# Reordering the start-up of a one-core feature-attention and ternary feed-forward kernel on Trainium2

## The reference

```
def _rfs(xw, ab, AB, gs):
    dot_products = jnp.einsum('...d,rd->...r', xw, ab[:, None] * gs)
    correction = (0.5 * jnp.sum(xw * xw, axis=-1))[..., None] * (ab * ab)
    return 1.0 / math.sqrt(NUM_RFS) * AB * jnp.exp(dot_products - correction)
...
weights = _rfs(input_weights, ab, AB, proj_matrix)
feats = _rfs(x, ab, AB, proj_matrix)
return jnp.einsum('bsr,or->bso', feats, weights)
...
h = jax.nn.silu(_tlin(x, w1_w, w1_s)) * _tlin(x, w2_w, w2_s)
h = jax.nn.gelu(_tlin(h, h1_w, h1_s), approximate=False)
h = jax.nn.gelu(_tlin(h, h2_w, h2_s), approximate=False)
return _tlin(h, w3_w, w3_s)
```

## Time and profile before

| | |
|---|---|
| median of 3 runs | 1315.86 us |
| lowest, highest | 1315.18, 1316.37 us |
| profiled execution | 1315.81 us |
| its span | 1314.0 us |
| TensorE busy with products | 1290.7 us (98%) |
| VectorE, ScalarE, GpSimd busy | 947.4, 750.7, 742.1 us |
| granted TensorE clock, mean | 0.998 |

### The profile page before, as it was taken

How to read it: one execution, slowest core, us unless ns; L and a number is a source line. 1 busy time by engine, 2 the same in 40 slices (tenths; PEclk the granted TensorE clock), 3 DMA queues, 4 the chain that set the end, 5 groups by cost and what they waited for, 6 DMA issues and landing times. The chain is left out here.

```text
span 1314.0 us, 16120 instructions
## 1 busy us (share of the span) xinstructions
PE 1290.7 (98%) x6068; PEld 1067.9 (81%) x6068; DVE 947.4 (72%) x1195; ACT 750.7 (57%) x1004; POOL 742.1 (56%) x705
## 2 busy tenths in 40 slices
PE   6999999999999999999999999999999999999997
PEld 5788888888888888888878888788897888878887
DVE  7887759677587875877758786687857777466575
ACT  3556644666456664566644656456554575555664
POOL 7952014789558994589935998369982791020000
PEclk9999999999999999999999999999999999999999
DMA  9787734654255452555416544274542754313441
GB/s 338 268 314 230 267 97 117 196 175 152 102 133 196 152 180 77 147 169 177 161 69 168 179 148 163 80 185 150 174 133 81 188 177 131 110 64 128 136 166 38
DMA packets 96836, 207.50 MB, mean 158 GB/s; under 512 B 13936, under 2 KB 16240, under 8 KB 95728
## 3 DMA queue, kind: packets, MB, share of 16 engines
q1 hardware_dynamic: 80032, 157.11, 35.9%
q0 software_dynamic: 16720, 49.30, 13.7%
HBM read 174.87 MB, written 37.78 MB: 162 GB/s over the span
## 5 line engine op out<-in xcount | busy, mean ns | idle before, releaser
L218 PE MATMUL ps<-split,ring 128*128 128x512 f32 x2800 | 763.6, 390 | 0.0
L218 PEld LDWEIGHTS ps<-split,ring 128*128 128x128 f32 x2800 | 525.6, 188 | 109.1
L201 DVE TENSOR_TENSOR split<-quad,split 128x1024 fp32r<-128x1024 f32 x258 | 341.8, 1335 | 186.1 <-ACT split L197 185.0
L221 PE MATMUL ps<-split,ring 128*128 128x512 f32 x784 | 305.0, 389 | 0.0
L197 ACT ACTIVATE split<-quad 128x1024 fp32r<-128x1024 f32 x258 | 266.4, 1052 | 42.4 <-PE ps L221 42.3
L218 PE MATMUL ps<-xT,w 128*128 128x512 f32 x768 | 220.3, 395 | 7.6 <-DVE quad L211 6.0
L579 POOL TENSOR_TENSOR cube<-cube,seen 128x256 f32<-128x256 f32 x176 | 206.6, 1174 | 14.3
L197 ACT ACTIVATE quad<-ps 128x512 f32<-128x512 f32 x193 | 114.5, 596 | 118.7 <-PE ps L221 118.0
L218 PEld LDWEIGHTS ps<-xT,w 128*128 128x128 f32 x768 | 143.3, 188 | 43.7 <-DVE quad L211 9.3
L197 ACT ACTIVATE quad<-quad,cols 128x512 f32<-128x512 f32 (+1 forms) x194 | 137.6, 717 | 66.3 <-DVE quad L201 64.0
L201 DVE TENSOR_TENSOR quad<-quad 128x1024 f32<-128x1024 f32 x128 | 173.0, 1391 | 0.0
(11 more groups left out here) (96 smaller groups left out, 1172.9 us busy)
## 6 DMA issues: line engine op xcount, KB each, us to landing
ring<-hs SPq DMA_DIRECT2D x428, 256.0 KB, 3.5
xin<-in_x SPq DMA_DIRECT2D x17, 512.0 KB, 3.2
s_h<-s SPq DMA_DIRECT2D x16, 512.0 KB, 6.3
seen<-in_h POOLq DMA_DIRECT2D x64, 128.0 KB, 2.8
ry<-in_x SPq DMA_DIRECT2D x15, 512.0 KB, 5.5
out<-ry SPq DMA_DIRECT2D x15, 512.0 KB, 2.6
hs<-in_h SPq DMA_DIRECT2D x6, 1024.0 KB, 7.7
z_h<-xin POOLq DMA_DIRECT2D x48, 128.0 KB, 4.4
```

The lines of the kernel that those rows point to most:

```text
L201: return dve.mark(lambda e: e.tensor_tensor(dst, a, b, op))
L218: pe.run(lambda e: e.matmul(dst, stat, mov, start=start, stop=stop, skip_group_check=loose))
L221: return pe.mark(lambda e: e.matmul(dst, stat, mov, start=start, stop=stop, skip_group_check=loose))
```

## The change

Sixteen products of `ident` with itself go to bank 1 at TensorE's very start; nobody reads them. `turn_rows` hands back its two copies over `xin` as a function, to be called later. For step 0 of half 0 the four products with the high parts come first, for both banks, and only then the wait for the low parts. `turn_rows(0)` uses banks 0 and 1. `norms_win`, the copy of `wt` and `dots_win` move from ahead of the first tile into `side` of half 0. The statistics of half 1 go three tasks a step (two in step 0), `turn_rows(1)` goes from step 7 to step 5, its copies to step 6, `turn_norms_win` from step 1 to 3 and `exponents_win` from step 2 to 4. SyncE waits for the first rows and the projections before it issues the second rows, and issues `w3s` after the norms' store of half 0. `features_win` comes ahead of `dots(0)`, and its scaling is done by ScalarE.

```
+WARM = 16
@@ turn_rows
-                hi = cast(xT[j][:, kd, 0, :], ps[:, banks[kd], :], turned[kd], *xT_free.get(h - 2, []))
+                hi = xT_hi[h] = cast(xT[j][:, kd, 0, :], ps[:, banks[kd], :], turned[kd], *xT_free.get(h - 2, []))
                 xT_lo[h] = vv(xT[j][:, kd, 1, :], ps[:, banks[kd], :], xT[j][:, kd, 0, :].bitcast(F32), ALU.subtract, hi)
+            return lambda: copy_rows(h, banks, turned[-1])
+
+        def copy_rows(h, banks, tok):
             for kd in range(KD):
-                xTf_done[h] = vcopy(xTf[j][:, kd, :], ps[:, banks[kd], :], turned[-1])
+                xTf_done[h] = vcopy(xTf[h % 2][:, kd, :], ps[:, banks[kd], :], tok)
                 free[banks[kd]] = [xTf_done[h]]
@@ gated_step
-            pe.wait(xT_lo[h], *w12_ready(m), *free[pair[0]])
-            a = group(ps[:, pair[0], :], [(w1[:, k, m * P:(m + 1) * P], xT[j][:, k, g, :]) for k in range(KD) for g in range(2)])
-            pe.wait(*free[pair[1]])
-            b = group(ps[:, pair[1], :], [(w2[:, k, m * P:(m + 1) * P], xT[j][:, k, g, :]) for k in range(KD) for g in range(2)])
+            pe.wait(xT_hi[h], *w12_ready(m), *free[pair[0]])
+            parts = [[[(w[:, k, m * P:(m + 1) * P], xT[j][:, k, g, :]) for k in range(KD)] for g in range(2)] for w in (w1, w2)]
+
+            if h == 0 and m == 0:
+                pe.wait(*free[pair[1]])
+                for n in range(2):
+                    group(ps[:, pair[n], :], parts[n][0], True, False, True)
+                pe.wait(xT_lo[h])
+                a, b = (group(ps[:, pair[n], :], parts[n][1], False, True, True) for n in range(2))
+            else:
+                pe.wait(xT_lo[h])
+                a = group(ps[:, pair[0], :], parts[0][0] + parts[0][1])
+                pe.wait(*free[pair[1]])
+                b = group(ps[:, pair[1], :], parts[1][0] + parts[1][1])
@@ loads
+        sp.wait(d_x[0].token, d_pj.token)
...
         load_x(1)
-        d_w3s.send(sp, w3s[:, 0, :], w3s_in)
-        d_w3s.send(sp, w3s[:, 1, :], w3s_in)
@@ turn_win
-            made_w["wt"] = cast(wt, two, tok)
+            made_w["turned"] = tok
+
+        def copy_win():
+            made_w["wt"] = cast(wt, ps[:, 3, :].rearrange("p (a b) -> p a b", a=2), made_w["turned"])
@@ dots_win
-            pe.wait(made_w["PT"], made_w["wt"])
+            pe.wait(made_w["PT"], made_w["wt"], *free[0])
@@ features_win
-                f = vs(WS[:, r, :], WF[:, r, :], amp[:, 2, r:r + 1], None, ALU.mult, None, e, made_w["b2"])
-                ws_done[0] = f
+                ws_done[0] = cast(WS[:, r, :], WF[:, r, :], e, made_w["b2"], func=ACT.Copy, scale=amp[:, 2, r:r + 1])
@@ ahead of the first tile
         pe.wait(c_ident)
+        for _ in range(WARM):
+            mm(ps[:, 1, 0:P], ident[:, :], ident[:, :], True, True)
...
-        norms_win()
-        turn_rows(0, (4, 5))
-        dots_win()
+        copy_first = turn_rows(0, (0, 1))
@@ tile 0
-                side = {m: stats1[2 * m:2 * m + 2] for m in range(KH)}
-                side[1].append(turn_norms_win)
-                side[2].append(exponents_win)
+                side = {m: stats1[3 * m - 1:3 * m + 2] for m in range(1, KH)}
+                side[0] = [copy_first, copy_win] + stats1[:2]
+                side[1].append(norms_win)
+                side[2].append(dots_win)
+                side[3].append(turn_norms_win)
+                side[4].append(exponents_win)
                 norms_out(0)
-                side[7] += [lambda: turn_rows(1, (0, 1)), lambda: norms_in(0)]
+                d_w3s.send(sp, w3s[:, 0, :], w3s_in)
+                d_w3s.send(sp, w3s[:, 1, :], w3s_in)
+                copies1 = []
+                side[5] += [lambda: copies1.append(turn_rows(1, (0, 1))), lambda: norms_in(0)]
+                side[6].append(lambda: copies1[0]())
...
                 norms_in(1)
+                features_win()
                 dots(h0, (4, 5), L0.at["v"])
-                features_win()
                 dots(h1, (6, 7), L0.at["v"])
```

More of the change, by code:

```diff
@@ L650, in turn_win @@
                 tok = turn(ps[:, 3, kd * D:(kd + 1) * D], wi, kd, KD)
-            two = ps[:, 3, :].rearrange("p (a b) -> p a b", a=2)
-            made_w["wt"] = cast(wt, two, tok)
+            made_w["turned"] = tok
+        def copy_win():
+            made_w["wt"] = cast(wt, ps[:, 3, :].rearrange("p (a b) -> p a b", a=2), made_w["turned"])
             free[3] = [made_w["wt"]]
@@ L988, in between @@
                 if t == 0 and n == 0:
-                    turn_rows(h0 + 2, (4, 5))
+                    turn_rows(h0 + 2, (4, 5))()
                 if t == 0 and n == 2:
-                    turn_rows(h1 + 2, (6, 7))
+                    turn_rows(h1 + 2, (6, 7))()
                 if n == 2 and t + 1 < NT:
```

## The result

The changed kernel takes 1318.51 us (median; 1316.38 to 1320.81), the kernel before 1315.99 on the same chip (1314.14 to 1318.89). The ratio of their times is 1.0019, with a 95% interval of 1.0012 to 1.0026: a little slower, 2.5 us. The profiled execution of the changed kernel took 1319.73 us, with a span of 1317.8.

What follows compares the result with a forecast made beforehand. VectorE, its operations stretched, was taken to set when the first half ends. The sum (4.7 - 4.0) + 0.8 = 1.5 us, less 0.2 for late-landing weights, gave 1.3 us and 1314.6 us, range 1311.9 to 1317.3.

Steps and rivals of the forecast that it cites:

- S: First half: lengthening of VectorE's operations, mainly beside GpSimd's additions; taken as 4.0 us, between 0 and the 6.7 of before.
- rival C: First half: VectorE's operations stretch as before, S = 6.7; 1.2 us slower, 1317.1; chance 0.10.
- Second half: Gated layer: its second half starts from about 33.4, 4.7 us less S sooner than 34.11.
- The start: First gated product at 11.3 in place of 13.60, with the high parts first.
- The features: Mixing follows the dot products at once, at 55.62 in place of 56.34; gain 0.8 us.
- The new wait: TensorE waits 4.4 us (sign: 3 to 6) for VectorE's exponents ahead of turning the second rows.
- the four old ones: TensorE's first-half waits, thrice for `quad` or `xin`, once for `xT`, 4.3 us; most goes into one new wait.
- B: VectorE does nearly all its SBUF work before GpSimd adds, S 0.5 to 2.5; gain about 3.7, 1312.2; chance 0.28.
- A: The main forecast, S = 4.0 in the first half: 1314.6, own range 1313.2 to 1316.2; chance 0.54.
- D: Second rows landing after 13.1 lengthen VectorE's chain; from 17.0 over 0.2% slower, at 17.5 1319.0; chance 0.05.
- E: What is gained is lost later, where the products wait for VectorE's sums: 1315.9; chance 0.03.
- The skill's rule: VectorE instructions with two SBUF inputs are blocked only by GpSimd instructions reading SBUF; S 2.9, whole gain 2.6 us.

Runs made afterwards that it cites:

- loads as before: The changed kernel with SyncE's wait taken out, so the second rows and `w3s` are issued at once as in the kernel before: 1317.06 us, ratio 1.0002.
- additions later: The changed kernel with GpSimd's first addition held until VectorE has normalised the second rows: 1311.81 us, ratio to the kernel before 0.9979.
- the exponents first: The changed kernel with the weights' norms and exponents ahead of the second pair of normalisations of the second rows, in step 3: 1316.27 us, ratio 1.0003.
- the turning at step 7: The changed kernel with the second rows turned ahead of step 7 instead of step 5: 1313.54 us, ratio to the kernel before 0.9986.
- the start alone: The kernel before with only the 16 unread products and step 0's high parts first: 1314.73 us, ratio 0.9988.

## Why the prediction was wrong

The race in one table: when VectorE's chain begins (the copies) and how long it is, up to the end of the exponents; when the additions begin; the wait. S is the chain less the 11.0 that I had counted (10.4 + 0.63); with one long operation left it is 1.4, so some 0.3 of each S is no stretching but my count.

| kernel | copies | additions | chain | S | wait at the turning |
|---|---|---|---|---|---|
| changed, first profile | 13.26 | 19.40 | 18.04 | 7.0 | 7.37 |
| changed, once more | 11.95 | 18.30 | 19.54 | 8.5 | 8.95 |
| changed, no unread products | 13.33 | 19.03 | 20.33 | 9.3 | 7.69 |
| changed, loads as before | 12.12 | 20.55 | 15.71 | 4.7 | 4.83 |
| changed, additions later | 12.03 | 21.39 | 12.44 | 1.4 | 1.80 |

- **The step that failed is the stretching S = 4.0.** It measured 7.0 and 8.5, both above the end that I had kept for rival C (6.7). I had the additions at 19.4 and VectorE through the Newton steps at 19.0. The additions came at 19.40 and 18.30. At the same moments VectorE had six of the nine Newton operations still to do, where I had none: in the first profile because the chain began at 13.26 and not 11.9, in the second because it was caught 2 us earlier, in the weights' norms. I had bounded S above by its value of before, though the change makes GpSimd start sooner and puts more operations into the chain; so 6.7 was no upper end.
- **The second term was missing: the clock.** I let TensorE idle for 4.4 us and priced what comes behind at the fast rate (0.1 + 1.0 + 5.4). From 31.30 to 39.27 it took 8.0 us in place of 6.5. The earlier trace rows had both levels; I used them for the start and not for the wait. The experiment that kept TensorE at work took 6.5 for the same stretch.
- **The sum of the first profile.** Second half predicted at 33.4. The first gated product came 1.3 us late and with it the copies (+1.36), S was 3.0 over, the clock took 1.6 as counted at the top: 39.4, measured 39.27. In the second profile: start as predicted, S 4.5 over, and the clock 2.2: 40.2, measured 40.23. Without the clock's 1.5 the median would be about 1317.0, an estimate: inside the whole range, but still slower than the kernel before, where I had forecast it faster.
- **The start held,** though not in the first profile: 12.57 there, but 11.25 to 11.72 in six others with the same start and loads (the repetition and the five edits of the changed kernel that leave both as they are). In the first, the projections landed at 7.8 and not 6.4 (ScalarE's scaling begins at 7.81 and 6.38), and a wait of 0.55 for `wi` follows. That was chance of the loads, and I had given the start no range of its own. The unread products end at 8.1, in time, but what they are worth I had under-read: they keep the gated layer's first products off the low level, and with that VectorE's chain from coming later still under the additions. Without them the kernel is 5.3 us slower.
- **The features held:** 0.7 us of the 0.8, in the changed kernel and alone.
- **The new wait held in kind, place and cause,** and the four old ones are gone as said. Its two parts in the first profile: VectorE's end at 31.30 instead of 26.9, less a TensorE that reached the turning 1.4 us later than 22.6 (4.4 + 4.4 - 1.4 = 7.4). That its forecast of 4.4 was not further off is partly luck: the late start of that execution held TensorE up too.
- **The rivals.** C was the right one, with 0.10 of the chance, and too mild: it gave 1317.1. B needed the Newton steps to escape; it happened in the profile of the exponents first, where VectorE ended them at 19.21 and the additions began at 19.38. The changed kernel misses it by one to two microseconds, by the table. I gave A and B 0.82 together on arithmetic with no more margin than that. D was hardly seen: the statistics of the second rows (14.46) follow the copies without a pause; only with the turning at step 7 VectorE waited for these rows, 0.23 us. E neither in the changed kernel: from 67.37 on it loses nothing, and gains 0.4 us behind the last product.
- **The skill's rule.** By it (the Trainium skill, "SBUF — State Buffer", "Who interferes with whom") the issuing of loads would not hold VectorE, and S would be 2.9. The measurement is against the 2.9. On the rule itself the runs say something between: long operations do begin 1.0 to 1.5 us ahead of the first addition (19.13, with the addition at 20.43; 17.34 with 18.30 above; 19.04 with 20.55 with the loads as before), yet where the additions were put off, alone, the loads went on to 20.27, and Newton operations at 19.18 and 19.37 took 0.16 us. So there the loads alone didn't hold VectorE, as the page says. What does is open: it came only where GpSimd went from its loads to the addition without waiting, and in two of these three cases the held operation ended 0.1 to 0.4 us before the addition is recorded to start (19.13 + 1.15 and 20.43; 19.04 + 1.15 and 20.55). Which operations are held agrees with the page for those with two inputs in SBUF and for the gated results, which have one in PSUM and are not held. The normalisations have one tensor as input, in SBUF, and are held too; the sentences used here do not cover them.

## What to carry to other kernels

When a wait is concentrated in one place, ask what the one awaited chain shares with an engine that the same change makes earlier, and how many operations of it are left at that moment; if the answer hangs on a microsecond or two, it is a race and not a number, and an explicit wait that takes one side out of it (here GpSimd's first addition: 3.4 us in the kernel before, and the changed kernel from 2.5 us slower to 3.4 faster) is worth more than an order that hopes to win. An idle time of TensorE of some microseconds can cost again behind its end, at the lower clock (1.5 us here); and work moved out of a pause early in the kernel may have been what kept the clock up.

## What the runs showed of the hardware

- **Small VectorE operations last until GpSimd's addition is over.** An operation on four numbers per partition, 0.16 us by itself, mostly takes 1.11 to 1.59 while GpSimd adds (0.78 to 2.39 in all), and ends within 0.04 us of the addition that it met (for the first hold see below); its neighbours with one input in PSUM keep their 0.75. The normalisations, 0.41 by themselves, are held too (up to 1.96). GpSimd's first four additions take about as long in every profile (5.36 to 5.60), so beside these operations the loss is one-sided. It is not so everywhere: later, beside VectorE's subtractions of 128x1024, four such additions took up to 8.03 (from 39.40 in the changed kernel).
- **The first hold begins ahead of the addition's record,** by 1.0 to 1.5 us in the three cases named above. Where GpSimd waited before its first addition (additions later in three kernels, and 0.50 us for a load with the exponents first), no operation was held ahead of it. That an engine waits for something that the trace does not show was the largest surprise; its cause is open.
- **The clock can fall after a short pause.** With the start alone, TensorE paused for 1.87 us before 26.93, and from 28.00 on the granted clock was 0.50 for 3.41 us, though TensorE was busy throughout. The window's row (columns as above):

```profile
28.00:31.41 3.41, 3.41 (x14) 3.02 (x13) 3.15 (x5) 1.12 (x3) 3.24 (x3) 0.50 1.32 387
```

  The same followed the 1.78 us ahead of 84.33, the 1.90 ahead of 83.91 and, with the turning at step 7, the 2.38 ahead of 29.57. It does not always follow, and the length of the pause does not decide it: the additions later had a pause of 1.80 us before 24.53, a little longer than the 1.78 of the same execution, and the clock stayed at 1.00; so it did in the kernel before behind the 1.64 before 34.11, from 34.10 to 63.10. What decides is not shown. The row behind the 1.80:

```profile
24.53:31.00 6.47, 6.47 (x33) 5.51 (x34) 4.50 (x7) 3.20 (x6) 6.00 (x7) 1.00 1.30 398
```

- **A small gap in the loads moves much.** The projections landed at 6.4 in one profile and 7.8 in another of the same kernel. That moves the first gated product by 1.3 us and the wait by 1.6, in the other direction: where the start was 1.3 us sooner, the additions began 1.1 sooner too, VectorE's chain ended 0.2 later all the same (31.49 against 31.30), and TensorE was there 1.4 us sooner to wait for it.
